# An attention, feed-forward and mixture-of-experts block: the first batch's tokens are chosen inside the tile loop, and four experts run batch by batch on raw fp32 weights

## The chip, the cores and the metric

One core of a Trainium2 chip. The time is that of one execution on the device, in microseconds. The engines: PE (TensorE, matmul), DVE (VectorE), ACT (ScalarE), POOL (GpSimd) and SP (SyncE, which here only issues DMAs). Each engine takes its instructions in the order of the program and waits at semaphores for the others.

## The reference

Two batches of 2048 rows of 512 values (x) pass four residual blocks; each begins with a layer norm.

```python
x = x + xattn0(layernorm(x), ctx, ctx, mask, ...)   # q, k, v and scores with relu, no softmax
x = x + ffn0(layernorm(x), weight, bias)            # input and weight rounded to blocks of fp6
x = x + xattn1(layernorm(x), ctx, W, b)             # a matmul and a mean of ctx
x = x + moe(layernorm(x), Wg, bg, w1, ..., b3)

# moe, for each of 16 experts e and each batch b
probs = softmax(x @ Wg + bg, axis=-2)               # over the 2048 rows
vals, idx = top_k(probs.T, 128)                     # 128 rows for each expert
h = relu(tok @ w1[e] + b1[e]); h = relu(h @ w2[e] + b2[e]); h = h @ w3[e] + b3[e]
outputs[b, idx] += h * vals                         # tok = x[b, idx]
```

Each expert takes the 128 rows of each batch that it rates highest. An expert's top rows aren't known before the last of the batch's 2048 rows has its logits.

## The kernel before

Rows are worked on in N = 32 tiles of 128; tiles 0 to 15 are the first batch. A loop over k = 0 to 35 is software-pipelined, written once for each engine: iteration k quantises tile k (`quantise`), adds the feed-forward result of tile k-1, mixes tile k-2 (`mix` on PE), and ends tile k-3 (`second_residual` on DVE). Ahead run the q projection (`q_chunk`), `scores` for groups of four tiles, and `attend(k+1)` with `first_residual(k+1)`. Each residual is followed by its statistics (bn_stats and bn_aggr on DVE, or sums on ACT), from which POOL makes a reciprocal root (`rstd_of`). DVE also takes the low part of each value that goes through PE in three passes: a value is split in a high and a low part (fp32r), and a product is high x high, high x low and low x high (`three_passes`, L250). `xdT_l` is that low part for the quantised tile, and the feed-forward matmuls `ffn(k)` wait for it. Some choices of order depend on k: from tile 24 on `attend(k+1)` stands ahead of the transposes `t2(k)` (`ahead`), and at k = 27 behind the mix (`mix_first`).

Each group of four tiles writes its logits into `seg`: a row for each batch, expert and quarter of 512 rows, 128 rows in all; the first batch's are rows 0 to 63 and complete in iteration 19. The normed rows go to the tensor xn4 in DRAM, the sums of the first three blocks to out.

Behind the loop each engine waits for all of this (`phase1_over`). Then DVE chooses: 16 rounds of max, max_index and match_replace give the 128 largest of each row of 512; the four quarters are brought into one row by a DMA (`cand`) and merged by a bitonic network (L1486 to L1513). PE turns ids and values (L789, L791), and POOL gathers the tokens by indirect DMA (L1714). The expert stage takes expert by expert, both batches together, 256 tokens: `hidden(e, 0)`, the transposes of the next expert's tokens, `outputs(e-1)`, `hidden(e, 1)`. Weights, 1 MB for a layer, come by DMA into `w_raw`, ACT and DVE split them into `w_h` and `w_l`. The results are added to out by an indirect DMA on POOL (L1725). `keep_warm` are matmuls whose result nobody reads.

## Time and profile before

| | |
|---|---|
| median of 3 runs | 786.26 us (785.6 to 787.0) |
| profiled execution | 786.69 us |
| its span, first to last instruction | 784.9 us |
| PE busy | 698.9 us (89%) |
| DVE busy | 554.4 us (71%) |
| ACT busy | 446.6 us (57%) |
| POOL busy | 436.5 us (56%) |
| mean granted clock of PE | 0.954 |
| moved by DMA | 103.04 MB, mean 131 GB/s |

The span is what the trace covers; the execution's own time is 1.8 us longer. The granted clock is a share of 2.4 GHz and has two levels, 1.00 and 0.50. Busy shares are means over stages that are quite different, so the sections below go by stage.

### The profile page before, as it was taken

Reading aid. Unit: us, or ns where it says so; the run is one execution under the profiler, and the core shown is the slowest. Engines: PE = TensorE matmul, PEld = TensorE weight load, DVE = VectorE, ACT = ScalarE, POOL = GpSimd, SP = SyncE. Lnnn points to the kernel's source line nnn. Section 1 sums busy time; section 2 is a strip of 40 time slices with the busy share of each in tenths; the row PEclk is TensorE's granted clock in tenths of the full one; section 3 lists DMA queues with packets and bytes.
Section 4 is the critical chain, followed back from the end, with each engine's and each line's share of the span. In section 5 each row is a group of like instructions: output and inputs, shape, how many; then the busy total and the mean of one; then the engine's idle time right before and its main releaser. Section 6 shows DMA issues by size and latency. Waiting matters only on the chain.

```text
span 784.9 us, 12400 instructions
## 1 busy us (share of the span) xinstructions
PE 698.9 (89%) x4357; PEld 617.7 (79%) x4357; DVE 554.4 (71%) x918; ACT 446.6 (57%) x750; POOL 436.5 (56%) x596
## 2 busy tenths in 40 slices
PE   6999999999999999999883007999999999999993
PEld 5766888888888888888772006999999999999993
DVE  5787588788787978777775984576666767677741
ACT  5754677777777676545352203656566666665640
POOL 2635788888888888877672603044444333334321
PEclk9999999999999999999897557999999999999998
DMA  8600122222212221111114144278888878777742
GB/s 306 236 28 14 42 95 67 83 68 83 81 56 96 68 87 52 65 45 56 41 70 158 71 167 126 91 225 242 240 247 235 236 239 238 234 226 220 216 66 35
DMA packets 54093, 103.04 MB, mean 131 GB/s; under 512 B 5392, under 2 KB 6672, under 8 KB 54032
## 3 DMA queue, kind: packets, MB, share of 16 engines
q1 hardware_dynamic: 46864, 85.47, 33.3%
q0 software_dynamic: 7168, 16.78, 9.6%
q8 instruction: 35, 0.57, 0.3%
q14 instruction: 26, 0.21, 0.1%
HBM read 76.68 MB, written 25.17 MB: 130 GB/s over the span
## 4 chain that ended last, share of the span: by engine, by line
PE 54%; DVE 13%; ACT 11%; issue 9%; POOL 9%; DMA 2%; POOLq 0%; SPq 0%; ACTq 0%; DVEq 0%
PE bank L250 31%; PE banks L250 12%; PE bank L257 4%; ACT xn L927 3%; POOL rstd_all L1603 3%; DVE bn L1155 2%; DVE x L1316 2%; PE banks L571 2%; PE banks L577 1%; DVE pack L1432 1%; DVE left L1439 1%; ACT qT_h L960 1%; DVE pos L1434 1%; POOL x L1690 1%; POOL xd L1682 1%
## 5 line engine op out<-in xcount | busy, mean ns | idle before, releaser
L1725 POOL DMA_INDIRECT out<-y,ids x32 | 76.2, 2380 | 173.6 <-DVE y L1552 169.0
L1167 DVE TENSOR_TENSOR w_l<-w_raw,w_h 128x2048 fp32r<-128x2048 f32 x45 | 103.0, 2290 | 31.2 <-ACT w_h L871 30.0
L1118 ACT ACTIVATE h<-bank,b 128x512 f32<-128x512 f32 x64 | 44.0, 687 | 107.5 <-PE bank L250 107.5
L871 ACT ACTIVATE w_h<-w_raw 128x2048 fp32r<-128x2048 f32 x48 | 90.6, 1924 | 5.3 <-DMA w_raw<-w 5.3
L1167 DVE TENSOR_TENSOR hT_l<-h,hT_h 128x512 fp32r<-128x512 f32 x64 | 44.2, 691 | 66.9 <-ACT hT_h L1124 66.9
L250 PE MATMUL bank<-hT_h,w_l 128*128 128x256 f32 x256 | 72.4, 283 | 0.0
L250 PE MATMUL bank<-hT_h,w_h 128*128 128x256 f32 x256 | 72.4, 283 | 0.0
L250 PE MATMUL bank<-tokT_h,w_h 128*128 128x256 f32 x256 | 72.4, 283 | 0.0
L250 PE MATMUL bank<-tokT_l,w_h 128*128 128x256 f32 x256 | 72.4, 283 | 0.0
L250 PE MATMUL bank<-hT_l,w_h 128*128 128x256 f32 x256 | 72.4, 283 | 0.0
L250 PE MATMUL bank<-tokT_h,w_l 128*128 128x256 f32 x256 | 72.4, 283 | 0.0
L1155 DVE BATCH_NORM_STATS2 bn<-x 128x6 f32<-128x512 f32 x79 | 54.6, 691 | 7.5 <-DMA x<-x 5.2
L1714 POOL DMA_INDIRECT tok<-xn,ids x32 | 31.9, 998 | 47.6 <-DVE ids L1522 29.4
L250 PE MATMUL bank<-wf_h,xdT_h 128*128 128x512 f32 x128 | 53.0, 414 | 0.8 <-DVE xdT_l L1167 0.8
L250 PE MATMUL banks<-w_h,hT_h 128*128 128x512 f32 x128 | 51.2, 400 | 0.0
L250 PE MATMUL bank<-wf_h,xdT_l 128*128 128x512 f32 x128 | 50.3, 393 | 0.0
L250 PE MATMUL bank<-wf_l,xdT_h 128*128 128x512 f32 x128 | 50.0, 391 | 0.0
L250 PE MATMUL banks<-w_h,hT_l 128*128 128x512 f32 x128 | 49.9, 390 | 0.0
L250 PE MATMUL banks<-w_l,hT_h 128*128 128x512 f32 x128 | 49.8, 389 | 0.0
L250 PEld LDWEIGHTS bank<-hT_l,w_h 128*128 128x128 f32 x256 | 49.1, 192 | 0.6
L250 PEld LDWEIGHTS bank<-hT_h,w_h 128*128 128x128 f32 x256 | 49.1, 192 | 0.6
L250 PEld LDWEIGHTS bank<-tokT_h,w_h 128*128 128x128 f32 x256 | 49.1, 192 | 0.2 <-issue 0.2
(249 smaller groups left out, 2233.1 us busy)
## 6 DMA issues: line engine op xcount, KB each, us to landing
w_raw<-w SPq DMA_DIRECT2D x48, 1024.0 KB, 6.9
x<-x SPq DMA_DIRECT2D x32, 256.0 KB, 2.8
out<-x SPq DMA_DIRECT2D x32, 256.0 KB, 2.0
xn<-xn SPq DMA_DIRECT2D x32, 256.0 KB, 2.0
mask<-mask_t SPq DMA_DIRECT2D x8, 256.0 KB, 3.1
stage<-wk SPq DMA_DIRECT2D x1, 1024.0 KB, 7.9
stage<-wq SPq DMA_DIRECT2D x2, 512.0 KB, 7.9
stage<-wf SPq DMA_DIRECT2D x1, 1024.0 KB, 10.9
```

The costliest lines, as they stand in the source:

```text
L250: last = pe.matmul(out, a, b, start=(n == 0), stop=(n == 3 * len(pairs) - 1))
L257: last = pe.transpose(bank[:, c * P:(c + 1) * P], src[:, c * P:(c + 1) * P], ident[:, :])
L571: last = pe.matmul(both_halves[:, a, 0:WIDE], xh[:, d, :], wc_h[:, d, a, :], start=(d == 0), stop=(d == C - 1))
L871: act.activation(dst, src, ACT.Copy).then_inc(sem, 1)
L927: act.activation(spare[:, :], src[:, :], ACT.Copy, scale=-1.0 / D, accum_out=m[:, 0:1]).then_inc(sm.a_sum, 1)
L1118: act.activation(h32[n % 2][:, :], ps_hid[n % 4][:, :], ACT.Relu, bias=bias)
L1155: dve.bn_stats(bn6[which][:, j % 2, :], src[:, :]).then_inc(sem_bn[which], 1)
L1167: dve.tensor_tensor(dst, src, hi_part, ALU.subtract).then_inc(sem, 1)
L1316: dve.scalar_tensor_tensor(x1[j % 2][:, :], ps_av[:, :], 0.0, x_in[j % XR][:, :], ALU.max, ALU.add)\
L1603: pool.tensor_tensor(inverse, r[:, 0:1], eps_exp[:, :], ALU.pow).then_inc(sem, 1)
L1714: pool.indirect_dma_start(out=tok[e % 2][:, b, :], out_offset=None, in_=io.xn4, in_offset=bass.IndirectOffsetOnAxis(ap=ids[:, r:r + 1], ax ...
L1725: pool.indirect_dma_start(out=out_rows, out_offset=bass.IndirectOffsetOnAxis(ap=ids[:, r:r + 1], axis=0), in_=y[e % 2][b][:, :], in_offset ...
```

## The change

The first batch's choice moves into the loop. `top_step(0, n)`, n = 0 to 47, are the 48 instructions of the 16 rounds on rows 0 to 63: five in each of the iterations 20 to 27, then 3, 3 and 2. `load_cand(0)` brings the lists together, and the merge's ten steps stand in iterations 31 (three), 32 (three) and 33 (four). The ids are turned in iterations 34 and 35, and the first four tokens' gathers are issued before `phase1_over` is passed or right behind it. The statistics of the third residual of tiles 19 to 30 (`THIRD`) are made on ACT (`sums3`) instead of on DVE. `mix_first` goes: attend(28) and first_residual(28) stand where they do in the other iterations, and quantise(28) comes first in its iteration on DVE.

The second batch's choice stays behind the loop, on rows 64 to 127 alone.

Experts 0 to 3 no longer go through three passes. They run batch by batch in 24 units (2 batches, 4 experts, 3 layers; `gap_of`), two experts alternating. A unit is four transposes, a copy to SBUF on ACT (`gap_in`), four fp32 matmuls of 128x512 with the weights as they come from DRAM (`gap_layer`), and an eviction on ACT (`gap_out`). The first 12 units belong to the first batch. Each unit loads its weights anew, so 24 loads where the four experts had 12; four are issued in iterations 28 to 31. Experts 4 to 15 run as before (ES = 12). keep_warm of the expert stage goes, and the last outputs begin with the first two of four chunks while the others are still made (`last_outputs`).

```diff
+    THIRD = range(19, 31)
+    STEPS = 3 * TOP // 8
+    def steps_of(k):
+        if 20 <= k < 28:
+            return range(5 * (k - 20), 5 * (k - 19))
+        return {28: range(40, 43), 29: range(43, 46), 30: range(46, STEPS)}.get(k, [])
+    def gap_of(n):
+        return n // 12, 2 * (n // 6 % 2) + n % 2, n // 2 % 3, n % 2
...
+        def load_gap(n):
+            b, e, layer, s = gap_of(n)
+            if n >= 4:
+                sp.wait_ge(sm.p_gl, n - 3)
+            else:
+                sp.wait_ge(sm.p_q, N)
+            sp.dma_start(gw[n % 4][:, :, :], chunked(io.w[layer][e])).then_inc(sem_gw[n % 4], 16)
...
         for i in range(RAW):
             load_raw(i)
-        sp.wait_ge(sm.k_top, 1)
-        sp.wait_ge(sm.a_soft, 1)
-        sp.dma_start(cand[:, :, :], pack[:, :]).then_inc(sm.k_cand, 16)
-        for i in range(RAW, len(order)):
+        for n in range(4, 10):
+            load_gap(n)
+        load_cand(1)
+        for n in range(10, 14):
+            load_gap(n)
+        for i in range(RAW, 2 * RAW):
+            load_raw(i)
+        for n in range(14, GAP):
+            load_gap(n)
+        for i in range(2 * RAW, len(order)):
             load_raw(i)
...
+        gap_turn(0)
+        for n in range(GAP):
+            gap_layer(n, 0)
+            if n + 1 not in (12, GAP):
+                gap_turn(n + 1)
+            gap_layer(n, 1)
+            if n + 1 == 12:
+                ids_turned(1, ps[1])
+                vals_turned(1, ps[0])
+                gap_turn(12)
+            if n == GAP - 2:
+                tokens(0)
+        for e in range(ES):
             hidden(e, 0)
-            if e == 0:
-                keep_warm(8, wh, ps_y[0])
...
             if parts_of(k) is not None:
                 logit_parts(parts_of(k))
+            for n in steps_of(k):
+                top_step(0, n)
+            if k == 30:
+                top_closed(0)
             if valid(k):
                 dve.wait_ge(sm.a_hi2, k + 1)
                 lo(sm.d_lo2, xd_l[:, :, :], in4(ps_tb), xd_h[:, :, :])
...
-            if not ahead(k) and valid(k + 1) and not mix_first(k):
+            if k == N - 1:
+                merge_open(0)
+                for i in range(3):
+                    merge_step(0, i)
+            if not ahead(k) and valid(k + 1):
                 first_residual(k + 1)
```

The order on DVE in iteration 20, from the add of tile 19's feed-forward result to the statistics of tile 21's first residual. Before:

```order
L1391 TENSOR_TENSOR x_1_125<-bank,x_1_134 128x512
L1155 BN_STATS bn_71<-x_1_125 128x6
L1160 BN_AGGR mean_var_67<-bn_71 128x2
L1167 TENSOR_TENSOR xdT_l<-bank,xdT_h 128x512
L1316 SCALAR_TENSOR_TENSOR x_1_134<-bank,x_98 128x512
L1155 BN_STATS bn_70<-x_1_134 128x6
L1160 BN_AGGR mean_var_66<-bn_70 128x2
L1330 SCALAR_TENSOR_TENSOR x_0_140<-banks,rstd_all_54,x_0_124 128x512
```

Now (the numbers in names differ from program to program):

```order
L1750 TENSOR_TENSOR x_1_133<-bank,x_1_142 128x512
L1611 MAX pack<-seg_logits 64x8
L1619 TENSOR_SCALAR negm<-pack 64x1
L1621 MATCH_REPLACE left_153<-pack,seg_logits 64x512
L1611 MAX pack<-left_153 64x8
L1615 MAX_INDEX pos<-pack,seg_logits 64x8
L1407 TENSOR_TENSOR xdT_l<-bank,xdT_h 128x512
L1558 SCALAR_TENSOR_TENSOR x_1_142<-bank,x_106 128x512
L1395 BN_STATS bn_70<-x_1_142 128x6
L1400 BN_AGGR mean_var_66<-bn_70 128x2
```

The statistics behind the add are gone, and five steps of the choice (the small negm belongs to the third) stand between the add and xdT_l.

The order on DVE in iteration 24, where `attend` and the first residual stand ahead. Before:

```order
L1316 SCALAR_TENSOR_TENSOR x_1_134<-bank,x_102 128x512
L1155 BN_STATS bn_70<-x_1_134 128x6
L1160 BN_AGGR mean_var_66<-bn_70 128x2
L1167 TENSOR_TENSOR xdT_l<-bank,xdT_h 128x512
L1339 TENSOR_REDUCE amax<-xc 128x16
```

Now:

```order
L1558 SCALAR_TENSOR_TENSOR x_1_142<-bank,x_110 128x512
L1395 BN_STATS bn_70<-x_1_142 128x6
L1400 BN_AGGR mean_var_66<-bn_70 128x2
L1621 MATCH_REPLACE left_153<-pack,left_152 64x512
L1611 MAX pack<-left_153 64x8
L1615 MAX_INDEX pos<-pack,left_152 64x8
L1621 MATCH_REPLACE left_154<-pack,left_153 64x512
L1611 MAX pack<-left_154 64x8
L1407 TENSOR_TENSOR xdT_l<-bank,xdT_h 128x512
L1585 TENSOR_REDUCE amax<-xc 128x16
```

The five steps stand between the new statistics and xdT_l, for which PE's next ffn waits.

The order on PE where the loop ends: lg_t are the last logits, top_i and top_v ids and values, tok the tokens. Before:

```order
L789 MATMUL bank<-ident,top_i 128x32
L791 MATMUL bank<-ident,top_v 128x32
L470 MATMUL banks<-w_h_186 128x512 x7
L257 MATMUL bank<-ident,tok_196 128x128 x8
L470 MATMUL banks<-w_h_186 128x512 x8
```

Now, from the values of the first batch on:

```order
L833 MATMUL banks<-ident,top_v_194 128x16
L289 MATMUL bank<-ident,gap_tok_176 128x128 x4
L932 MATMUL bank<-gap_w_202,gap_xT_178 128x512 x2
L289 MATMUL bank<-ident,gap_tok_177 128x128 x4
L932 MATMUL bank<-gap_w_202,gap_xT_178 128x512 x2
L932 MATMUL bank<-gap_w_203,gap_xT_179 128x512 x2
L289 MATMUL bank<-ident,gap_h_180 128x128 x4
L932 MATMUL bank<-gap_w_203,gap_xT_179 128x512 x2
```

And at the border of the two batches:

```order
L932 MATMUL bank<-gap_w_205,gap_xT_179 128x512 x4
L828 MATMUL bank<-ident,top_i_197 128x16
L833 MATMUL bank<-ident,top_v_195 128x16
L289 MATMUL bank<-ident,gap_tok_176 128x128 x4
L932 MATMUL bank<-gap_w_202,gap_xT_178 128x512 x2
```

Units follow each other on PE, the transposes of the next in the middle of each; the ids of the second batch are turned behind the twelfth unit, and its first tokens behind them.

## Rows read from the trace of the kernel before

**Rows 1.** Stages: start:end, us, busy us of PE, PEld, DVE, ACT, POOL, clock, DMA, GB/s.

```profile
281.94:327.07 45.13, 45.02 (x263) 39.04 (x262) 36.14 (x66) 28.30 (x60) 37.45 (x61) 1.00 0.21 70
327.07:367.72 40.65, 40.07 (x235) 35.14 (x234) 30.29 (x60) 20.62 (x44) 32.66 (x52) 1.00 0.15 56
367.72:425.57 57.85, 44.51 (x262) 38.93 (x260) 38.65 (x79) 22.54 (x50) 33.70 (x61) 0.92 0.18 65
425.57:479.96 54.39, 3.92 (x9) 2.50 (x9) 46.22 (x148) 7.24 (x7) 16.87 (x7) 0.50 0.36 127
479.96:772.87 292.91, 292.87 (x2076) 275.71 (x2076) 186.67 (x172) 176.36 (x205) 103.13 (x60) 1.00 0.72 205
```

**Rows 2.** The chain that ended last, expert stage: start us, us, what.

```profile
483.50 5.75 PE bank L250 x48
...
491.96 11.52 PE bank L250 x96
503.48 0.87 PE bank L257 x8
504.35 5.47 PE banks L250 x24
...
764.64 2.75 PE bank L470 x12
```

**Rows 3.** Timeline of the hole: start us, us, engine, instruction, [idle before].

```profile
425.57 0.69 DVE L1432 MAX8 pack<-seg_logits 128x8 f32<-128x512 f32 x1 [3.31 <-DMA seg_logits<-lrow]
...
457.79 0.29 DVE L1444 TENSOR_SCALAR pack<-pos,segbase 128x128 f32<-128x128 uint32 x1
460.96 0.15 DVE L1449 TENSOR_REDUCE gmax<-cand 32x1 f32<-32x4 f32 x1 [2.89 <-DMA cand<-pack]
...
474.76 0.28 PE L789 MATMUL bank<-ident,top_i 32*128 32x32 f32 x1 [52.15 <-DVE es L1516]
...
479.96 1.38 PE L257 MATMUL bank<-ident,tok 128*128 128x128 f32 x5 [0.38 <-DMA tok<-xn,ids]
```

**Rows 4.** Source line 619: duration ns, first and last start us, forms.

```profile
L619 PE MATMUL banks<-stage,ctx_raw x8: 592/592/595, 33.7 to 36.7; 128*128 128x512 f32 x8
```

**Rows 5.** Three short stretches, columns as in rows 1.

```profile
372.30:375.40 3.10, 0.00 (x0) 0.00 (x0) 2.96 (x7) 1.24 (x3) 2.47 (x6) 1.00 0.01 3
375.40:382.20 6.80, 6.09 (x27) 6.09 (x28) 4.80 (x11) 1.35 (x3) 4.99 (x9) 0.50 0.11 41
...
476.30:481.20 4.90, 4.53 (x13) 3.10 (x14) 0.00 (x0) 0.08 (x1) 3.46 (x4) 0.50 0.54 144
```

**Rows 6.** Timeline of DVE in iteration 20 of the tile loop.

```profile
286.81 0.68 DVE L1391 TENSOR_TENSOR x<-bank,x 128x512 f32<-128x512 f32 x1
...
288.26 0.18 DVE L1160 BATCH_NORM_AGGREGATE mean_var<-bn 128x2 f32<-128x6 f32 x1
290.26 0.69 DVE L1167 TENSOR_TENSOR xdT_l<-bank,xdT_h 128x512 fp32r<-128x512 f32 x1 [1.81 <-ACT xdT_h L871]
...
292.53 0.75 DVE L1330 SCALAR_TENSOR_TENSOR x<-banks,rstd_all,x 128x512 f32<-128x512 f32 x1
```

**Rows 7.** Timeline of DVE and PE in iterations 24 and 25.

```profile
333.67 0.69 DVE L1316 SCALAR_TENSOR_TENSOR x<-bank,x 128x512 f32<-128x512 f32 x1 [1.22 <-PE bank L250]
...
343.70 0.69 DVE L1316 SCALAR_TENSOR_TENSOR x<-bank,x 128x512 f32<-128x512 f32 x1 [1.77 <-PE bank L250]
...
337.26 0.48 PE L250 MATMUL bank<-wf_h,xdT_h 128*128 128x512 f32 x1
```

**Rows 8.** DMA issues (KB, us to landing), and a stretch with three loads.

```profile
w_raw<-w SPq DMA_DIRECT2D x48, 1024.0 KB, 6.9
...
430.50:433.70 3.20, 0.00 (x0) 0.00 (x0) 3.13 (x9) 1.91 (x1) 0.97 (x1) 0.50 1.04 391
```

**Rows 9.** Timeline of DVE: the same instruction in two iterations.

```profile
355.30 1.08 DVE L1297 TENSOR_TENSOR lg_sum<-lt 128x128 f32<-128x128 f32 x1
...
420.86 0.27 DVE L1297 TENSOR_TENSOR lg_sum<-lt 128x128 f32<-128x128 f32 x1
```

More of the change, by code:

```diff
@@ L58, in build @@
     SEG = G * E
-    ROWS = B * E
+    NG = 4
+    ES = E - NG
     CB = B * KEYS
@@ L124, in build @@
     wgf = place("wg_pair", [P, C, 2 * E])
-    ids = place("ids", [P, ROWS], U32)
-    vals = place("vals", [P, ROWS])
+    ids = place("ids", [P, B * E], U32)
+    vals = place("vals", [P, B * E])
+    b3v = place("b3_vals", [P, B * E])
+    negm = place("negm", [P, 1])
+    gmax = [place(f"gmax{b}", [E, 4]) for b in range(B)]
+    eg = [place(f"eg{b}", [E, GB]) for b in range(B)]
+    es = [place(f"es{b}", [E, GB]) for b in range(B)]
     phase_base = top[0]
@@ L166, in build @@
     xn4 = [place(f"xn4_{i}", [P, D]) for i in range(2)]
+    left = [place(f"left{i}", [P, GT]) for i in range(3)]
+    pos = place("pos", [P, TOP], U32)
+    pack = place("pack", [P, 2 * TOP + 1])
+    assert top[0] <= at_cd + 16 * 1024
     top[0] = at_cd + 16 * 1024
@@ new lines, in build @@
+    exps = place("exps", [P, GT], at=at_xn1)
+    spot = [at_q32]
+    top_v = [more(f"top_v{b}", [E, TOP]) for b in range(B)]
+    top_i = [more(f"top_i{b}", [E, TOP]) for b in range(B)]
+    y = [[more(f"y{i}{b}", [P, D]) for b in range(B)] for i in range(2)]
+    assert spot[0] <= at_xt1
+    gw = [place(f"gap_w{i}", [P, C, D], at=at_xt1 + 8 * KB * i) for i in range(4)]
+    w_h += [place(f"w_h{3 + i}", [P, C, D], F32R, at=at_xt1 + 8 * KB * i) for i in range(2)]
+    w_l += [place(f"w_l{3 + i}", [P, C, D], F32R, at=at_xt1 + 8 * KB * (2 + i)) for i in range(2)]
@@ L217, in banks @@
+    h32 = [more(f"h32_{i}", [P, 2 * B * P]) for i in range(2)]
+    h_h = [more(f"hT_h{i}", [P, C, B * P], F32R) for i in range(2)]
+    h_l = [more(f"hT_l{i}", [P, C, B * P], F32R) for i in range(2)]
+    assert spot[0] <= at_cd + 8 * KB, (spot[0], at_cd + 8 * KB)
     def banks(*names):
@@ L765, in _ @@
                 t2(k)
-            if valid(k + 1) and not ahead(k) and not mix_first(k):
+            if valid(k + 1) and not ahead(k):
                 attend(k + 1)
@@ L1352, in quantise, with top_step @@
                 .then_inc(sm.d_q8, 1)
+        def top_step(b, n):
+            rows = rows_of(b)
+            r = n // 3
+            now = (seg if r == 0 else left[r % 3])[rows, :]
+            eight = pack[rows, 8 * r:8 * r + 8]
+            if n == 0 and b == 0:
+                for i in range(2):
+                    dve.wait_ge(sem_seg[i], 16 * (G // 4))
+            if n % 3 == 0:
+                chain[0] += 1
+                dve.max(eight, now).then_inc(sm.d_chain, 1)
+                max_at[0] = chain[0]
+            if n % 3 == 1 and r >= 1:
+                last = (seg if r == 1 else left[(r - 1) % 3])[rows, :]
+                dve.max_index(pos[rows, 8 * r - 8:8 * r], pack[rows, 8 * r - 8:8 * r], last)
+            if n % 3 == 2:
+                dve.wait_ge(sm.d_chain, max_at[0])
+                if r == 0:
+                    dve.tensor_scalar(negm[rows, :], pack[rows, 0:1], -1.0, None, ALU.mult).then_inc(sm.k_exp, 1)
+                if r + 1 < TOP // 8:
+                    then(dve.match_replace(left[(r + 1) % 3][rows, :], eight, now, LOWEST))
+                else:
+                    then(dve.max_index(pos[rows, 8 * r:8 * r + 8], eight, now))
@@ L1556, in _ @@
         nxt = AHEAD
-        for e in range(E):
+        for e in range(ES):
             if nxt < len(order):
```

548 lines of the change are left out of this document (373 added, 175 removed).

## The prediction

> **What bounds the kernel now.** I read the busy time by stage first, then the chain that ended last, then the rows of single stages.
>
> [Rows 1] give three kernels in one. In the tile loop PE is busy 45.02 of 45.13 us over four tiles, so PE sets the pace; DVE is busy 36.14 of them. Between 425.57 and 479.96 PE works 3.92 us of 54.39: everything waits for the choice of the tokens, on DVE. From 479.96 PE is busy 292.87 of 292.91 us, the DMA engines 0.72. The reader should see that PE has one hole, and that DVE, whose work the hole waits for, still has some room in the loop.
>
> In the expert stage the chain is PE alone, 11.52 + 0.87 + 5.47 = 17.86 us an expert [rows 2]; warm-up matmuls stand in front of the last outputs (2.75 us).
>
> In the hole [rows 3]: 48 steps of eight, from 425.57 to 457.79, 0.671 us each; lists in another layout by DMA at 460.96; after the merge PE turns the ids at 474.76; the gathered tokens are on PE at 479.96. That is 54.39 us for both batches together. Each instruction is charged by elements in a row, not by rows, so I take one batch alone (64 rows for 128, 16 lists for 32) at the same time. That is a choice; no row shows an instruction on fewer partitions against the same one on more.
>
> **The change part by part, against the profiled span of 784.9 us** (786.69 us as a run, 0.4 over the median).
>
> *Fewer three-pass experts.* Four of sixteen go: 4 x 17.86 = **-71.4**. The warm-up matmuls go too: before the last outputs 2.75, behind the first hidden layer eight more (about 1.8, by the same 0.23 us each). Splitting the last outputs by halves lets their first half, 2.7 us, hide the ReLU and the low part of the second: **-4.6**, and +0.3 because both batches' results now end closer together.
>
> *Raw fp32 layers.* A layer is four transposes and four 128x512 fp32 matmuls. Eight hardware passes for four such matmuls start from 33.7 to 36.7 [rows 4], 0.43 apart, so 3.43 us; eight transposes take 0.87 [rows 2], so four 0.43. A unit is 3.86 us on PE; four experts, two batches, three layers make 24 units, 92.6 us, more than the 71.4 they replace. The gain is only in where they lie. ACT's copies fit: the turn of the next unit stands in the middle of a layer, 1.7 us away from either end, and two evictions take about 0.7 each.
>
> *First batch: hidden.* Its 12 units run while DVE chooses for the second. They end at 0.8 + 12 x 3.43 + 11 x 0.43 + the cold clock. The granted clock was 0.50 after the loop and came back 4.9 us after PE resumed [rows 5]; I charge 2.5 us. With about 1 us of start that is 50.1 us after the loop. The second batch's ids come at 0.9 (DVE now first waits for PE's turn of the first values) + 49.2 [rows 3]. So it is a tie: nothing is exposed, nor is there any cover left. From here each us that the first 12 units lose is an us of the total. I add **+1.2** for the 0.9 and the tie.
>
> *Second batch: exposed.* Its ids are as late as before, then 12 units run where before the experts began. Before, 3.5 us lay from the first transposes to the first hidden layer at 483.50 [rows 2]. Now 0.4 + 0.8 + 12 x 3.43 + 11 x 0.43 = 47.1, + 0.9 for the tokens of the first normal expert. PE also idles 4.8 us for the gather. An idle of 3.84 us in the loop brought the clock to 0.50 for 6.8 us [rows 5], so I charge 2.5 again: 50.5 - 3.5 = **+47.0**.
>
> *The tile loop.* DVE gets 48 steps and the first merge; twelve bn_stats/bn_aggr pairs move to ACT, which has 17 us free over four tiles. Iteration 20: the pair ended at 288.44, then DVE waited 1.81 for ACT before xdT_l, and x of the next tile began at 292.53 [rows 6]. Now five steps (3.36) begin at 287.5 where the pair stood: -0.95 + 3.36 - 1.81 = +0.6. Over iterations 20 to 23 DVE needs 36.14 + 20 x 0.67 - 4 x 0.95 = 45.8 of 45.13 us, plus waits that steps can't fill. Walked row by row I get **+1.9**.
>
> From iteration 24 attend(k+1) stands ahead, and the steps lie between the new first residual and xdT_l, on which PE's next ffn waits. The old period is 343.70 - 333.67 = 10.03 [rows 7]. The new circle is: ffn start to first residual 343.70 - 337.26 = 6.44, the residual and its statistics 1.65, steps 3.36, xdT_l 0.7: 12.2. Three such iterations, **+6.6**. DVE's idle of 10.4 us in that stage [rows 1] doesn't help, since it waits for PE's attend ahead of the steps.
>
> Iterations 27 and 28: PE had idled 3.84 us and then ran 6.8 us at half clock [rows 5], because first_residual(28) stood behind the mix. Now it stands right behind xdT_l, but eight more steps do too: walked from xdT_l of tile 26, the transposes of tile 28 start as late as before (18.3 us on), the idle time in smaller parts. What goes is the half clock, 2.5 us over the mix; 1.0 is lost again where ffn(28) waits for xdT_l: **-1.5**. In iterations 29 and 30 the circle of [rows 7] still holds, with five steps and the close of the lists in it, 3.36 + 0.29, less 0.2: **+3.4**. Iterations 31 to 34 take the merge, 13.5 of the 13.8 us from 460.96 to 474.76 [rows 3]. DVE waits in them mostly for the last mixes (idle 19.2 of 57.85 us in this stage, [rows 1]). By my walk some 10 us of the merge fill such waits; its last four steps end 1.9 us behind the last mix, and 1.3 is lost before: **+3.2**. The merge can also be held by POOL. lg_sum took 1.08 us in one place and 0.27 in another [rows 9]; at the first a POOL tensor instruction ran beside it. In iterations 31 to 33 POOL has five long ones (three biases, xd, one x1), so 5 x 0.8 = 4 us at most, and I take **+1.0**.
>
> The Trainium skill (GPSIMD Engine Reference, section Key points) says that GpSimd shares its SBUF interfaces with VectorE, with contention for instructions that have two SBUF inputs. By it all of the merge's some 60 two-input instructions in the loop are exposed, and the search instructions, with one tensor input, are not; the trace agrees for lg_sum. If each of them met a POOL instruction the loop would grow by 60 x 0.8, some 48 us, and the kernel would be slower, 820.
>
> The loop in sum: 1.9 + 6.6 - 1.5 + 3.4 + 3.2 + 1.0 = **+14.6**. Bounds: all steps into idle time and only what exceeds it paid, some +4; and every step and merge paid in full, 48 x 0.67 + 13.5 - 12 x 0.95 = +34. I take the walk, as each of its terms names the instruction that waits.
>
> *Transfers.* 24 loads of 1 MB for four experts, since each batch loads them anew. Three loads ran at 391 GB/s (2.7 us each), landing 6.9 us after issue in the median [rows 8]. A unit needs 1.05 MB and a sixth of a megabyte of gathers and adds, 3.2 to 3.5 us of engines in 3.86. Four loads start in the loop, the others when a buffer is free, three units ahead (11.6 us for a landing of 6.9). I cost them at nothing; the cover is that 0.4 us a unit.
>
> **Sum:** 784.9 - 71.4 - 4.6 + 0.3 + 1.2 + 47.0 + 14.6 = 772.0; a run 1.8 more, against a median 0.4 lower: **773.4 us**.
>
> **The rivals.**
>
> *A. The loop absorbs the choice.* For it: DVE's idle, 9.0 and 10.4 us, covers the 9.6 net of four tiles, and iteration 28's stall returns 6 us. Against it: the wait for attend lies ahead of the steps. Loop +0 to +8, central 4: 763.
>
> *B. Slower: the weights feed doesn't keep up.* Between units a load must arrive every 3.86 us, 1.22 MB with its share of gathers and adds. The expert stage moved 205 GB/s at 0.72 [rows 1]. If something near 235 GB/s were the ceiling for this mix a unit would be 5.2 us, and as the tie leaves no cover all 24 pay: + 1.35 x 24 = 32, so 806. It decides from 0.54 us a unit, a unit of 4.4. Against it: 391 GB/s at the loads [rows 8].
>
> *C. The loop pays in full.* Every step lands on the path, +34, and idle PE brings the clock down again: 793. It decides from a stretch of 27. For it: DVE reaches 100% of the loop's pace; against: [rows 6] shows waits that steps fill.
>
> *D. The clock stays at 1.2 GHz in the fp32 units.* A unit would be 7.7 us, some +85. The fp32 rows ran at full pace [rows 4]. Nearly excluded.
>
> *E. Held by POOL.* Each instruction of the merge in the loop is held 0.8 us: 820, as five POOL instructions can't do; 0.01.
>
> *F. The clock never falls between the batches,* or the tie is won: 2 to 3 us less, within the range.
>
> By the Trainium skill (TensorE: Matmul & The Clock Gate, section HAM oscillation) gaps of idle throttle the engine again. By that rule the 4.8 us before the second batch costs what [rows 5] shows, and the sum already holds it; were PE's small waits in iterations 24 to 30 (0.7 to 2.5 us) enough, each would cost some 3 us more.
>
> **How the numbers follow.** My forecast, loop +8 to +21: 0.62. A 0.18. C, loop over +21: 0.08, a third of it still slightly faster or level. B and other stalls of the units: 0.10, a part of it (below 0.5 us a unit) still faster. D and E 0.02. A measurement of this kernel tells about 0.2% (1.6 us) from no change. Faster: 0.62 + 0.18 + 0.03 + 0.04 = 0.87; same 0.03; slower 0.10. The range takes in A's centre and the lower part of B and C: 761 to 785.
>
> **What the new profile would show.** PE busy in units of 3.9 us for some 50 us after the loop, a hole of 5 us, 47 us of units, then twelve periods of 17.86. The last logits landing near 440 instead of 425.57. In iterations 24 to 26 PE waiting about 2 us each for xdT_l. Wrong would be: transposes or fp32 matmuls waiting on gap_w (B), the loop ending before 433 (A) or after 447 (C), a search instruction that gets dearer or cheaper on 64 partitions.

## The result: slower by 1%, where 1.6% faster was forecast

Median 794.14 us (793.88 to 794.93, 4 runs) against 786.16 (785.6 to 787.0, 4 runs): ratio 1.0102, 95% interval 1.0085 to 1.0120. The profiled execution has a span of 791.8 us, where my sum gave 772.0. The page of the changed kernel:

```profile
span 791.8 us, 12063 instructions
...
PE 724.0 (91%) x4100; PEld 596.2 (75%) x4100; DVE 544.7 (69%) x1000; ACT 451.7 (57%) x807; POOL 429.4 (54%) x596
...
PEclk9999999999999999999989799789999999999997
```

I read the windows by stage next, against [rows 1]; columns as there.

```profile
292.52:332.22 39.70, 36.91 (x205) 31.58 (x204) 37.10 (x71) 25.13 (x57) 27.32 (x45) 0.96 0.14 48
332.22:370.82 38.60, 32.09 (x176) 27.35 (x174) 30.33 (x66) 21.44 (x47) 26.58 (x43) 0.96 0.13 48
370.82:387.01 16.19, 14.09 (x69) 12.25 (x70) 12.61 (x29) 6.67 (x15) 7.39 (x14) 0.89 0.29 100
387.01:420.35 33.34, 26.89 (x146) 23.31 (x144) 24.88 (x57) 16.54 (x39) 19.90 (x36) 0.90 0.43 142
420.35:451.64 31.29, 15.81 (x103) 13.65 (x104) 25.03 (x90) 11.11 (x27) 15.04 (x23) 0.89 0.25 87
451.83:512.56 60.73, 50.16 (x147) 24.55 (x147) 50.53 (x151) 23.41 (x40) 23.95 (x11) 0.89 0.95 318
512.56:563.65 51.09, 50.40 (x153) 25.23 (x153) 1.29 (x2) 15.98 (x25) 10.48 (x9) 0.93 0.76 242
```

The first five are the tile loop from iteration 21 on, then the first batch's units, then the second's. The reader should see two things. In the loop DVE is nearly full at first (37.10 of 39.70) and PE no longer is. And the last logits land at 451.64 instead of 425.57 [rows 3]; the second batch's tokens are on PE at 512.56:

```profile
451.64 0.25 PE L833 MATMUL banks<-ident,top_v 16*128 16x16 f32 x1 [4.60 <-DMA seg_logits<-lrow]
...
512.56 1.11 PE L289 MATMUL bank<-ident,gap_tok 128*128 128x128 f32 x4 [6.45 <-DMA gap_tok<-xn,ids]
```

Four stages against the forecast:

| stage | forecast | measured | miss |
|---|---|---|---|
| last logits landed | 440.2 | 451.64 | +11.5 |
| from there to the second batch's tokens on PE | 55.6 | 60.9 | +5.3 |
| from there to the first three-pass matmul | 50.5 | 51.1 | +0.6 |
| from there to the end | 225.7 | 228.1 | +2.4 |

### The profile page after: what moved, and what is told of

The parts are those of the page before. It is cut to its first block, busy times and chain, and to the rows that moved or that the text cites. A ratio compares the mean times of both kernels' runs of the same rounds, so it can differ in the third digit from the quotient of the medians.

```text
span 791.8 us, 12063 instructions
## 1 busy us (share of the span) xinstructions
PE 724.0 (91%) x4100; PEld 596.2 (75%) x4100; DVE 544.7 (69%) x1000; ACT 451.7 (57%) x807; POOL 429.4 (54%) x596
## 4 chain that ended last, share of the span: by engine, by line
issue 23%; PE 21%; DVE 18%; DMA 15%; POOL 11%; ACT 10%; POOLq 0%; DVEq 0%; ACTq 0%; SPq 0%
DMA out<-y,ids 13%; PE bank L282 7%; PE bank L932 5%; POOL rstd_all L1893 3%; PE bank L289 2%; ACT xn L1094 2%; DVE bn L1395 2%; DVE left L1621 2%; DVE pos L1615 2%; DVE pack L1611 2%; DVE x L1558 1%; PE banks L282 1%; POOL x L1980 1%; POOL xd L1972 1%; ACT qT_h L1153 1%
## 5 line engine op out<-in xcount | busy, mean ns | idle before, releaser
L2015 POOL DMA_INDIRECT out<-y,ids x24 | 56.2, 2341 | 131.4 <-DVE y L1837 127.7
L1407 DVE TENSOR_TENSOR w_l<-w_raw,w_h 128x2048 fp32r<-128x2048 f32 x33 | 75.6, 2290 | 26.5 <-ACT w_h L1038 26.5
L932 PE MATMUL bank<-gap_w,gap_xT 128*128 128x512 f32 x192 | 91.0, 617 | 1.5 <-ACT gap_xT L1308 1.5
L1407 DVE TENSOR_TENSOR hT_l<-h,hT_h 128x512 fp32r<-128x512 f32 x48 | 33.2, 691 | 50.9 <-ACT hT_h L1346 49.4
L932 PEld LDWEIGHTS bank<-gap_w,gap_xT 128*128 128x128 f32 x192 | 36.1, 199 | 37.6 <-issue 35.1
L1038 ACT ACTIVATE w_h<-w_raw 128x2048 fp32r<-128x2048 f32 x33 | 62.2, 1926 | 0.0
L282 PE MATMUL bank<-hT_h,w_h 128*128 128x256 f32 x192 | 54.3, 283 | 1.4 <-DVE hT_l L1407 1.4
L282 PE MATMUL bank<-wf_l,xdT_h 128*128 128x512 f32 x128 | 51.1, 399 | 0.0
L1034 ACT ACTIVATE xn<-x,rstd,rstd_all 128x512 f32<-128x512 f32 x32 | 26.2, 818 | 31.0 <-POOL rstd L1895 30.7
L1034 ACT ACTIVATE xn<-x,rstd 128x512 f32<-128x512 f32 x32 | 26.1, 816 | 30.9 <-POOL rstd L1901 24.8
L1904 POOL TENSOR_TENSOR qT_l<-q,qT_h 128x512 fp32r<-128x512 f32 x32 | 41.5, 1299 | 3.5 <-ACT qT_h L1153 3.5
L1407 DVE TENSOR_TENSOR xdT_l<-bank,xdT_h 128x512 fp32r<-128x512 f32 x32 | 21.9, 685 | 30.2 <-ACT xdT_h L1038 30.0
```

Source lines behind the costliest of these rows:

```text
L282: last = pe.matmul(out, a, b, start=(n == 0), stop=(n == 3 * len(pairs) - 1))
L932: last = pe.matmul(ps[4 + s][:, :], gx[s][:, d * P:(d + 1) * P], gw[n % 4][:, d, :], start=(d == 0), stop=(d == C - 1))
L1034: act.activation(dst[:, :], src[:, :], ACT.Identity, bias=r[:, n, 2:3], scale=scale)\
L1038: act.activation(dst, src, ACT.Copy).then_inc(sem, 1)
L1407: dve.tensor_tensor(dst, src, hi_part, ALU.subtract).then_inc(sem, 1)
L1904: pool.tensor_tensor(dst, src, hi_part, ALU.subtract).then_inc(sem, 1)
```

## The experiments

**Theories.** Mine after reading the trace, in two places. In the loop, the steps ahead of `xdT_l` keep PE's feed-forward waiting (9.7 us on the page where it was 0.8), and from iteration 28 the moved statistics stand in a circle through ACT and POOL. In the hole, one comparison of the second batch's merge took 4.19 us beside a split on POOL. Rivals: the changed order of PE and DVE did it; or DVE is simply full, so that no order helps; or the comparison was slow of itself.

All in all fourteen kernels. Each was timed beside the kernel before, whose median was 786.1 to 786.5 us every time, so their medians can be compared. late_choice and stats_back have one execution each. The yardstick in the loop is the start of `second_residual`, the add that ends tile k-3, one per iteration; the table gives the time between two of them, from the profiled execution of each kernel:

| | 21 to 24 | 24 to 27 | 27 to 28 | 28 to 31 | 31 to 34 | sum |
|---|---|---|---|---|---|---|
| before | 34.5 | 30.7 | 9.9 | 32.9 | 18.6 | 126.7 |
| after | 39.7 | 38.6 | 16.2 | 33.3 | 23.2 | 151.1 |
| late_choice | 33.9 | 31.1 | 15.8 | 33.3 | 20.1 | 134.1 |
| order_back | 39.7 | 38.6 | 14.5 | 37.0 | 23.2 | 153.0 |
| stats_back | 39.7 | 38.2 | 19.1 | 28.1 | 23.7 | 148.8 |
| stats_short | 39.4 | 38.7 | 19.1 | 28.1 | 23.7 | 148.9 |
| steps_behind | 39.7 | 33.3 | 15.8 | 33.3 | 23.4 | 145.4 |
| split_early | 39.6 | 40.2 | 19.0 | 33.3 | 25.3 | 157.5 |
| combined | 39.4 | 33.3 | 15.8 | 28.1 | 24.6 | 141.2 |
| combined_all | 41.5 | 32.7 | 16.0 | 28.1 | 23.8 | 142.0 |
| fewer_steps22 | 37.3 | 34.9 | 15.8 | 29.9 | 23.7 | 141.6 |

Split_early alters nothing in the loop, so its row against that of the changed kernel (after) tells how far two executions of one loop lie apart: 1.6 us in iterations 24 to 26, 2.9 in 27, 2.1 in 31 to 33, and next to nothing in 21 to 23 and 28 to 30. Smaller differences in those columns say nothing.

### late_choice: the choice taken out of the loop

```diff
-            for n in steps_of(k):
-                top_step(0, n)
...
         phase1_over(dve)
+        for n in range(STEPS):
+            top_step(0, n)
...
```

> The first batch's 48 steps, its merge and its turned ids and values stand behind the tile loop, ahead of the second batch's; everything else as in the changed kernel, the moved statistics and the altered order included. It is no candidate: it prices what the choice itself costs inside the loop. My theory: of the loop's +25.9 us, some 18 to 22 are the steps and the merge, and 4 to 8 are the moved statistics (the circle of iterations 28 to 31); so the loop ends 4 to 8 us behind the kernel before, at 429 to 434, and the profiled span is 791.8 - 25.9 + 6 + 55 (the first choice, exposed) = about 827. Rival: the moved statistics and the order cost most of it: the loop ends at 440 or later, and the span is 836 or more.

Span 826.3 us, as expected. DVE's first step starts right behind the last logits:

```profile
433.24 0.69 DVE L1603 MAX8 pack<-seg_logits 64x8 f32<-64x512 f32 x1 [3.51 <-DMA seg_logits<-lrow]
```

That is 7.7 us behind the kernel before. It is the price of what the change leaves in the loop without the choice: the moved statistics, the altered order and the four early loads; no run takes these apart. Its PE waits 0.7 us in all for `xdT_l`, like before. Against it the changed kernel is 18.4 us later (451.64), and that is the choice in the loop. Of the 17.0 us between the two rows of the table 13.3 lie in iterations 21 to 26, 3.1 in 31 to 33, and only 0.5 in 27 to 30, where the circle leaves DVE time anyway.

### steps_behind: the steps of iterations 24 on behind xdT_l

```diff
-            for n in steps_of(k):
+            for n in steps_of(k) if k < 24 else []:
                 top_step(0, n)
             if valid(k):
                 dve.wait_ge(sm.a_hi2, k + 1)
                 lo(sm.d_lo2, xd_l[:, :, :], in4(ps_tb), xd_h[:, :, :])
+            for n in steps_of(k) if k >= 24 else []:
+                top_step(0, n)
             if k == 30:
                 top_closed(0)
-            if valid(k):
-                dve.wait_ge(sm.a_hi2, k + 1)
-                lo(sm.d_lo2, xd_l[:, :, :], in4(ps_tb), xd_h[:, :, :])
```

> From iteration 24 the five steps stand behind VectorE's low part of the turned tile (xdT_l), on which TensorE's next feed-forward waits, instead of ahead of it. My theory: the steps then fill VectorE's wait for ScalarE's centred tile and TensorE's waits for xdT_l go, about 1 to 1.5 us in each of iterations 24 to 30: the loop ends 5 to 10 us earlier and the median is about 787. Rival: VectorE is simply full in iterations 22 to 27 and what it does not do here it does there: the loop ends within 2 us of the changed kernel's 451.6 and the median stays at 793 to 795.

788.5 us (787.53 to 789.82, 9 runs), 5.6 less than the changed kernel; ratio to the kernel before 1.0026 (1.0016 to 1.0037). Iterations 24 to 26 take 33.3 instead of 38.6 us, and PE's waits for `xdT_l` shrink. The rows of the two pages, after and steps_behind:

```profile
L282 PE MATMUL bank<-wf_h,xdT_h 128*128 128x512 f32 x128 | 54.4, 425 | 9.7 <-DVE xdT_l L1407 9.6
```

```profile
L282 PE MATMUL bank<-wf_h,xdT_h 128*128 128x512 f32 x128 | 53.1, 415 | 2.3 <-DVE xdT_l L1407 2.3
```

So place, not load, made 5.3 us of it: the same 15 steps cost 7.5 us ahead of `xdT_l` (38.6 against late_choice's 31.1) and 2.2 behind it. In iterations 28 to 30 nothing changed, so there the steps aren't what binds.

### stats_short and stats_back: the moved statistics

```diff
-    THIRD = range(19, 31)
+    THIRD = range(19, 27)
```

(stats_back leaves THIRD empty.)

> The third statistics of tiles 27 to 30 go back from ScalarE to VectorE; those of tiles 19 to 26 stay moved. My theory: in iterations 28 to 31 of the changed kernel the pace (11.1 us) is set by a circle through ScalarE's two sums and GpSimd's reciprocal root behind them, not by VectorE's load: the period of iterations 28 to 30 falls to 9.5 to 10.3 although VectorE has 0.95 us more in each, and the median falls by 2 to 5, to about 790. Rival: VectorE's load sets the pace there too, then each of the four iterations gets 0.9 us longer and the median is about 797.

> All twelve third statistics are back on VectorE; the steps and everything else as in the changed kernel. My theory: VectorE is full in iterations 20 to 27, so each of these grows by 0.7 to 0.95 us, some 6 in all, while iterations 28 to 31 lose the circle and get 3 to 5 shorter: 793 to 798 in total. Rival: VectorE was not what bound iterations 20 to 27, the moved sums on ScalarE and the reciprocal root at the end of GpSimd's turn were: then the loop ends 5 us or more earlier and the time is below 790.

792.07 (791.72 to 792.86) and 791.97 (one run). Both take 28.1 us for iterations 28 to 30 instead of 33.3, although DVE has more to do. So the moved statistics held these iterations, not DVE's load. The way that they do it I read from the rows of the changed kernel, around iteration 28:

```profile
391.83 0.27 POOL L1895 TENSOR_SCALAR rstd<-mean_var,rstd_all 128x1 f32<-128x1 f32 x1
392.13 0.81 ACT L1034 ACTIVATE xn<-x,rstd,rstd_all 128x512 f32<-128x512 f32 x1 [2.17 <-POOL rstd L1895]
392.85 0.61 ACT L1094 ACTIVATE v_bias<-x 128x512 f32<-128x512 f32 x1
393.59 0.73 ACT L1096 ACTIVATE v_bias<-x,mean_var 128x512 f32<-128x512 f32 x1
394.31 0.71 ACT L1207 ACTIVATE xc<-x,mean_var 128x512 f32<-128x512 f32 x1
394.49 0.19 POOL L1880 TENSOR_SCALAR rstd<-mean_var 128x1 f32<-128x1 f32 x1 [2.39 <-ACT v_bias L1096]
395.05 0.69 DVE L1585 TENSOR_REDUCE amax<-xc 128x16 f32<-128x512 f32 x1 [1.73 <-ACT xc L1207]
396.39 0.23 POOL L1899 TENSOR_SCALAR rstd<-rstd 128x1 f32<-128x1 f32 x1
```

POOL's root lets ACT norm; ACT's two sums (1.46 us) stand ahead of `xc`, for which DVE waits 1.73; POOL does the third root (from 394.49) ahead of the one that the quantising needs (396.39). Then DVE quantises, POOL makes xd and adds two biases, and the next root comes 11.1 us later. TensorE's clock, a rival for these 5.2 us, is not the cause: in the changed kernel iteration 28 took 11.14 us at a granted 1.00 and 29 took 11.11 at 0.85.

For iterations 20 to 26 my theory fell: stats_back puts 0.95 us per tile back on DVE there, and iterations 21 to 26 take no longer (39.7 and 38.2 against 39.7 and 38.6). Iteration 20 took 11.5 us instead of 10.5, but it took 11.2 in stats_short, which alters nothing there. By this one execution these statistics had been moved for nothing. In both kernels iteration 27 took 19.1 us against the changed kernel's 16.2; split_early, with the changed kernel's loop unaltered, shows 19.0 too, so that need not be the edit (see the last section).

### order_back: the order of iteration 27

```diff
-        return ahead(k) and k > N - 8
+        return ahead(k) and ahead(k - 1)
+    def mix_first(k):
+        return scores_of(k) is not None and not q_units(k)
...
```

> The two rules of order that the change altered are put back as they were: the attention of tile 28 behind the mix of iteration 27 on TensorE, its first residual at the start of the next iteration on VectorE, and the statistics of the last normalisation behind the quantising only where the tile before is ahead too. The steps and the moved statistics stay. My theory: order is not what cost the time; the half clock behind the long wait at iteration 27 comes back and the median is 794 to 797. Rival: the altered order is what stretches iterations 27 to 30, and the median falls by 4 to 8, to about 788.

795.76 us (793.31 to 797.75), 1.6 more, with overlapping ranges; iterations 27 to 30 take 51.5 us instead of 49.5, and 52.4 in split_early with the changed kernel's own order. The rival wanted 4 to 8 us less, so the order is not the cause; whether the new one is any better isn't shown.

### split_early: POOL's split ahead of the merge

```diff
         gap_add(0, 0)
+        split_lo(2)
         gap_add(0, 1)
-        split_lo(2)
```

> One line moved: GpSimd's low part of the third weight matrix stands ahead of the first batch's second scatter-add instead of behind it. My theory: in the changed kernel that split (486.86 to 491.93) held VectorE's first merge comparison of the second batch, 4.19 us instead of about 0.5 (488.02 to 492.21). Now the split should run from about 481.4 to 486.4, beside search instructions that read one tensor, and end ahead of the merge. The comparison takes about 0.5 us, the second batch's first unit starts at about 508.5 instead of 512.56, and the median falls by 4, from 794.1 to about 790. Rival: the comparison was slow because its lists had just landed by DMA, or because 16 partitions with strides are slow: it still takes 4 us and the time stays at 794.

The changed kernel, DVE and POOL:

```profile
488.02 4.19 DVE L1657 TENSOR_TENSOR ge<-cand 16x256 f32<-16x256 f32 x1
492.14 0.41 DVE L1663 TENSOR_TENSOR list_v<-cand 16x256 f32<-16x256 f32 x1
...
486.86 5.07 POOL L1904 TENSOR_TENSOR w_l<-w_raw,w_h 128x2048 fp32r<-128x2048 f32 x1
```

and split_early:

```profile
495.45 0.40 DVE L1657 TENSOR_TENSOR ge<-cand 16x256 f32<-16x256 f32 x1
...
488.13 4.51 POOL L1904 TENSOR_TENSOR w_l<-w_raw,w_h 128x2048 fp32r<-128x2048 f32 x1 [1.51 <-ACT w_h L1298]
```

4.19 against 0.40 us for the same instruction, the lists just landed in both: POOL's instruction held it until its own end at 491.93. In steps_behind and stats_short, where the split stands as in the changed kernel, it took 4.12 and 3.59. The first batch's units to the second batch's tokens take 57.15 instead of 60.73 us. The Trainium skill (SBUF — State Buffer, section SBUF: two separate sides) calls this an exclusive lock for the whole instruction and not a shared bandwidth; the trace agrees. The search steps ran on beside POOL's splits, 0.69 us as elsewhere. The median did not move (794.09, 792.62 to 797.13). In the profiled execution, the slowest of the four, iterations 21 to 33 took 6.4 us longer than in the changed kernel with the same loop, so a gain of 3.6 was not to be told in four runs. It stands by its rows, and by combined's, where the stretch from the last logits to these tokens is 57.1 us instead of 60.9.

### combined, combined_all, fewer_steps22

Combined is steps_behind, stats_short and split_early. Combined_all puts every step behind the first residual at the iteration's end; fewer_steps22 deals the steps out as `{20: 5, 21: 5, 22: 2, 23: 5, 24: 6, 25: 6, 26: 6, 27: 4, 28: 3, 29: 3, 30: 3}`.

> Three of the edits together: the steps of iterations 24 on behind xdT_l, the third statistics of tiles 27 to 30 back on VectorE, and GpSimd's third split ahead of the second scatter-add. If the causes are separate they add up: the loop ends at 451.6 - 4.1 - 3.5 = 444, the first unit of the second batch comes 57 us after the first of the first, and the median is 794.1 - 5.6 - 2.0 - 3.6 = 783, under the kernel before (786.3). Rival: the first two are one gain seen twice, as what iteration 26 gives back is lost in iterations 27 and 28: 786 to 788.

> As combined, but every step, those of iterations 20 to 23 too, stands behind xdT_l and behind the next tile's first residual and its statistics, at the end of VectorE's iteration. My theory: in iteration 22 TensorE waits 2.29 us for xdT_l behind three steps and then runs 4.29 us for 3.0 at half clock; these go, 3 to 5 us over iterations 20 to 23, and the median is 778 to 781. Rival: VectorE is full there in any case (11 us busy of 11.3) and the delay only moves on to the next tile's third residual: within 1.5 us of combined.

> Combined, with the 48 steps dealt out anew over iterations 20 to 30: 5, 5, 2, 5, 6, 6, 6, 4, 3, 3, 3 instead of 5 in each of the first eight and 3, 3, 2. Iteration 22 also has the three sums for the logits on VectorE; there the kernel without any step in the loop had a period of 10.5 us and combined one of 14.4. My theory: the steps ahead of xdT_l make TensorE wait and fall to half clock, so iteration 22 gets back 2 to 3.5 us; one step more in each of iterations 24 to 26 costs at most 0.7 us each, since they lie behind xdT_l: the loop ends 1.5 to 3 us earlier and the median is 777 to 778.5 against 779.9. Rival: VectorE is full from 20 to 27 whatever the order, and the three steps come back in full, so the time is the same within 1.

Combined: 779.92 us (779.13 to 781.39), ratio 0.9920 (0.9907 to 0.9934). The causes add up, and the kernel is faster than before. It gains 14.2 us on the changed kernel where the three by themselves make 11.2; in combined iteration 27 took 15.8 us, as in steps_behind, where the two others had 19.0 and 19.1. Combined_all: 783.11 (782.89 to 784.71), 3.2 worse: iteration 20 grows from 10.5 to 13.3 us and 21 to 23 from 39.4 to 41.5. Fewer_steps22: 781.0 (780.3 to 782.39). It wins 2.0 us where the steps left and loses 3.4 where they went. Its loop ends with combined's (the third residual of iteration 34 begins at 433.99 in both). So in iterations 20 to 23 DVE is full, another order doesn't help, and what leaves there is paid elsewhere: there the rival was right. Combined_all has no wait of PE for `xdT_l` there and is slower even so. 5.5 us of the choice stay (39.4 against late_choice's 33.9).

### warm_gap, raw_later: clock and transfers behind the hole

First warm_gap's edit to combined, then raw_later's:

```diff
                 vals_turned(1, ps[0])
+                pe.wait_ge(sm.a_w, 3)
+                keep_warm(22, w_h[2], ps[6])
                 gap_turn(12)
```

```diff
-        for n in range(10, 14):
+        for n in range(10, 18):
             load_gap(n)
         for i in range(RAW, 2 * RAW):
             load_raw(i)
-        for n in range(14, GAP):
+        for n in range(18, GAP):
             load_gap(n)
```

> Combined, with 22 matmuls of 512 columns that compute nothing needed, on TensorE between the turn of the second batch's values and its first tokens (some 4.8 us of the 6.5 us in which it is idle). It prices the term of 2.5 us for the clock behind that hole. My theory: the second batch's units run at full clock from the first on, the 51.8 us from the first transposes on become 49 to 49.5, and the median falls by 2 to 2.5, to 777.5. Rival: the idle time is not what lowers the clock (the fp32 units themselves are), or the added work reaches beyond the tokens' landing: then no gain.

> Combined, with the loads of the fourth to sixth three-pass weight matrices (3 MB) behind the second batch's first units' loads in SyncE's queue instead of ahead of them, issued at about 511 instead of 485.5. Combined's gather of the second batch's first tokens took 6.2 us from the copy of the ids to the transposes, with the DMA engines busy all the time. Theory: these 3 MB in flight delay the gather, so it takes 4.5 us, the second batch starts 1.5 to 2 us earlier and the median is about 778. Rival: the loads for the next units fill the DMA engines just as well: no change, or a unit of the second batch waits for its weights.

Both against combined. Warm_gap: 780.06 (779.36 to 781.03), no gain. The clock did stay at full; combined, then warm_gap:

```profile
499.20:504.00 4.80, 4.11 (x8) 2.12 (x9) 0.00 (x0) 0.60 (x1) 2.25 (x2) 0.50 1.05 387
```

```profile
500.50:505.00 4.50, 3.81 (x16) 2.07 (x16) 0.00 (x0) 1.19 (x2) 2.74 (x3) 1.00 1.04 387
...
510.65 1.96 PE L932 MATMUL bank<-gap_w,gap_xT 128*128 128x512 f32 x4 [0.77 <-issue]
515.85 0.67 PE L932 MATMUL bank<-gap_w,gap_xT 128*128 128x512 f32 x1 [1.08 <-issue]
```

The last two rows are waits inside units 14 and 15; combined has none there. They gave 1.85 us of it back, and the second batch's stretch, from its first transposes to the first three-pass matmul, took 50.3 us instead of 50.9. Raw_later: 787.17 (784.77 to 788.61), 7.3 worse. The gather was no faster (6.5 us from the copy of the ids to the transposes, combined 6.6), and a unit waited where the loads had moved to:

```profile
531.37 2.05 PE L932 MATMUL bank<-gap_w,gap_xT 128*128 128x512 f32 x2 [4.24 <-issue]
```

Behind that wait PE ran at a granted 0.58 for 6.7 us. My theory fell in this form: these three loads are not what holds the gather. The DMA share stayed at 1.05 during it (492.90 to 499.40), and loads put off from there are missed later.

### raw_early, raw_early_warm, one_early_warm

Raw_early issues the three loads ahead of those for units 8 and 10 and behind the lists; raw_early_warm adds 18 warm-up matmuls; one_early_warm has those and only the first of the loads early. Its edit of the loads:

```diff
         for n in range(4, 10):
+            if n == 8:
+                load_raw(RAW)
             load_gap(n)
...
-        for i in range(RAW, 2 * RAW):
+        for i in range(RAW + 1, 2 * RAW):
             load_raw(i)
```

> Combined, with the loads of the fourth to sixth three-pass weight matrices issued earlier: ahead of the loads for units 8 and 10 and right behind the lists, instead of one after the other at 485.5. In combined the DMA engines are busy 0.74 to 0.80 of the time from 462 to 482 and 1.04 to 1.07 from 482 to 522, across the gather of the second batch's tokens. My theory: transfers are a cost around that gather; with 3 MB moved into the quieter stretch the gather takes about 5 us instead of 6.1 and the median is 1 to 2 us under combined's 779.9. Rival: the loads only trade places, the stretch of 482 to 522 stays full, and the time is the same within 0.7.

> Raw_early and 18 matmuls that compute nothing needed in the wait for the second batch's tokens. With 22 of them and the old order of loads the clock stayed at full, but TensorE then waited 0.77 and 1.08 us inside units 14 and 15, and the second batch's stretch went only from 50.9 to 50.3. My theory: those waits were for weights behind a full set of DMA engines; with the earlier loads they go, the stretch is 48.5 to 49, and the median is 776 to 778. Rival: the waits were TensorE's own (the turn of the hidden rows behind ScalarE), they stay, and the time is that of raw_early.

> Combined, with 18 warm-up matmuls in the wait for the second batch's tokens and only one of the three weight loads earlier (ahead of unit 8's, at about 463); none is added between 466 and the lists' transfer at 476. In raw_early the lists' transfer took 10.4 us instead of 2.4, with some 6 MB issued in the 15 us ahead of it, while the gather fell from 6.1 to about 4 us. My theory: what is in flight at the moment a small transfer is issued sets how long it takes; here the lists take under 4 us and the gather 5 to 6, so the median is 778 to 780. Rival: any load moved into the first batch's units holds the lists, and the median is above 782.

Raw_early: 787.34 (785.43 to 789.58), 7.4 worse than combined. The second batch's lists, 64 KB, issued at 478.40, were there only at 488.77:

```profile
488.77 0.15 DVE L1647 TENSOR_REDUCE gmax<-cand 16x1 f32<-16x4 f32 x1 [12.07 <-DMA cand<-pack]
...
478.40 0.71 SPq L525 DMA_DIRECT2D cand<-pack  x1
```

In combined they took 2.4:

```profile
478.54 0.15 DVE L1646 TENSOR_REDUCE gmax<-cand 16x1 f32<-16x4 f32 x1 [2.47 <-DMA cand<-pack]
...
476.10 0.59 SPq L525 DMA_DIRECT2D cand<-pack  x1
```

The gather did fall, to 4.0 us from the copy of the ids. But it came so much later that most loads were through: the DMA share during it was 0.37, where it was 1.06 in combined. So this gain goes with the delay, and one load moved early alone (one_early_warm) didn't bring it.

Raw_early_warm: 786.27 (784.9 to 788.15). PE had idled 8.27 us just before the ids were turned; the warm-ups behind that ran at half clock for the most part (granted 0.50 until 506), 6.75 us for 18. The tokens' transposes began at 508.98, 7.2 us behind the copy of the ids instead of 4.0. One_early_warm: 777.79 us (776.98 to 778.15), ratio 0.9892 (0.9875 to 0.9908), the fastest kernel here:

```profile
500.00:547.90 47.90, 47.20 (x151) 23.70 (x152) 1.29 (x2) 15.97 (x25) 11.73 (x10) 1.00 0.84 271
...
494.78 4.39 PE L580 MATMUL banks<-w_h 128*128 128x512 f32 x18
500.01 0.66 PE L289 MATMUL bank<-ident,gap_tok 128*128 128x128 f32 x4 [0.84 <-DMA gap_tok<-xn,ids]
```

From the tokens to the first three-pass matmul 48.0 us, against combined's 50.9: the warm clock is worth 2.9 when the weights are there, as combined has no wait for weights in this stretch either. Its tokens came 0.8 us later, which leaves the 2.1 of the median. The lists took 2.4 us again, as I expected, but the gather 6.6 as in combined, not 5 to 6: the whole gain is the clock's. Why such warm-ups (22 of them) gave next to nothing in warm_gap I read as the one load that is now earlier, since the two waits in units are gone; it wasn't tried by itself. That loads issued shortly ahead of the lists hold them is shown for the orders tried, not where the bound lies. The Trainium skill (DMA: Bandwidth & Descriptors, section Queues, rings and completion order) has a transfer's completion land on each DMA engine only behind that engine's earlier writes. The 10.4 us agree with it, and would as well if the lists' own data had waited behind the loads; no run tells the two apart.

## Why the prediction was wrong

It failed in the step "The loop in sum: +14.6". The loop got 26.1 us longer, which is rival C's case by its size (over +21), to which I gave 0.08. It is not C's mechanism: C lets every step be paid, and late_choice shows 0.1 us for those of iterations 28 to 30. That C's 793 is so near the measured 794 is luck; it has +34 for the loop, and nothing for the hole. Where I wrote "by my walk" the prediction doesn't show the walk, so that for +1.9, -1.5 and +3.2 only the result of the step can be named. By the terms (starts of `second_residual` against before):

- **Iterations 20 to 23, +1.9: measured +5.2.** I let DVE be full (45.8 of 45.13 us) and still paid only 1.9, as if the steps could fill all but that little of its waits. The steps stand ahead of `xdT_l`. In iteration 22 the logit sums come ahead of them as well. DVE's and PE's rows and a window of PE's next matmuls there:

```profile
310.01 1.20 DVE L1538 TENSOR_TENSOR lg<-lg_sum,rstd_all 128x64 f32<-128x64 f32 x1
311.24 1.22 DVE L1540 TENSOR_TENSOR lg<-lg,lg_sum 128x64 f32<-128x64 f32 x1
...
316.98 0.50 PE L282 MATMUL bank<-wf_h,xdT_h 128*128 128x512 f32 x1 [2.29 <-DVE xdT_l L1407]
...
317.00:321.30 4.30, 4.30 (x13) 3.43 (x14) 4.13 (x8) 2.75 (x7) 2.28 (x4) 0.67 0.16 61
```

  Two sums took 1.2 us each where they take 0.23 elsewhere, PE waited 2.29 us, and its granted clock then was 0.67 on the mean of 4.3 us. late_choice, without steps, waits 0.7 us in all. Yet none of these three by itself makes the +5.2: in stats_back both sums take 0.23 us and the clock stays at 1.00, combined_all has no such wait, and iterations 21 to 23 take 39.7 and 41.5 us all the same. What these runs have in common is the steps on a nearly full DVE (busy 37.10 of 39.70 us here, 38.3 of 39.6 in stats_back); fewer_steps22, with three steps less in iteration 22, gets back 2.0 us, their own length.
- **Iterations 24 to 26, +6.6: measured +7.9.** Mechanism right, size nearly: PE waited 1.37, 1.91 and 3.12 us for `xdT_l`, where I had said about 2 each. steps_behind shows the place and takes 5.3 of it back.
- **Iterations 27 and 28, -1.5: measured +2.6.** Wrong in sign. I had credited 2.5 us for a half clock that goes. It didn't: the granted clock was 0.89 in iteration 27 and 0.90 in 28 to 30. late_choice has +2.1 there without a step, and split_early, with the same loop, 2.9 more for iteration 27. How the rest divides between the order and the moved statistics was not tried.
- **Iterations 29 and 30, +3.4: measured +4.1, by another cause.** I charged the steps. They cost nothing (late_choice has the same period of 11.1 us); the moved statistics, which I had taken as cost-free on ACT's 17 us of idle time, hold these iterations (stats_short takes 5.2 us less for 28 to 30). Idle time of an engine says nothing on whether it is idle at that place of the circle.
- **Iterations 31 to the end, +3.2 and +1.0: measured +6.3.** By late_choice 1.6 of it is not the merge. How the rest divides was not tried.

**The hole, "So it is a tie" and the 5.2 of the gather: +5.3.** The units themselves were right: 3.87 us each against 3.86. I looked for POOL's hold on the merge in the loop (E, +1.0) and not in the hole, where one split holds one instruction: +3.6 by split_early. The gather took 7.5 us from the turned ids instead of 5.2, beside DMA engines that are full (share 1.06; before, 0.38): +2.3. Together that is 5.9 for a miss of 5.3. That full DMA engines make the gather longer rests on these rows and on raw_early's 4.0 us at 0.37; no run changed that alone. "I cost them at nothing", said of the transfers, was right for the units of the changed kernel, which waited for no weights, and wrong for small transfers beside them.

**The second batch, +47.0: right** (51.1 against 50.5), the 2.5 us for the clock included: 2.9 by one_early_warm. Three-pass experts, -71.4 and -4.6: the last stage is 2.4 us longer than summed. The step that failed is the 1.8 credited for the eight warm-up matmuls behind the first hidden layer. They had stood in a wait that stays:

```profile
572.24 0.36 PE L282 MATMUL bank<-hT_h,w_h 128*128 128x256 f32 x1 [1.41 <-DVE hT_l L1407]
```

From the first three-pass matmul to the transposes of the third expert's tokens the changed kernel takes 20.17 us (563.65 to 583.82) and the kernel before, warm-ups included, 19.81 (483.50 to 503.31): +0.4 where the sum has -1.8.

Rival A (+0 to +8) is excluded: in combined, with the steps placed better, the loop still ends 16.5 us later than before, at 442.06. B did not occur, but raw_later (4.24 us in one unit) shows how near it lies. D and E did not occur; F only where warm-ups were added.

## What to carry to other kernels

Before work is put into a filled loop, ask not whether the engine has room but what waits behind the place: the same 15 steps cost 7.5 us ahead of the operand that TensorE waits for and 2.2 us behind it. Price each helping edit alone too: what the change left in the loop without the choice, statistics on another engine, a new order and early loads, cost 7.7 us and was credited with a gain. Warm-up matmuls that stand in a wait cost nothing, so taking the eight out gained nothing. Where a hole is filled with work that loads megabytes and splits weights, look at the small transfers and the two-input vector instructions on the path next to it: moving a few lines and adding 18 warm-up matmuls took this kernel from 794.1 to 777.8.

## What the runs showed of the hardware

- Search instructions on 64 partitions cost what they do on 128: 0.67 to 0.69 us for a row of 512 (MAX8, FIND_INDEX8, MATCH_REPLACE8), in split_early beside a 4.5 us split on POOL too. A comparison of two SBUF tensors took 4.19 instead of 0.40 us beside such a split.
- Where the clock falls differs between executions of the same loop. The same stretch of iteration 27 in the changed kernel and in split_early, whose loop is the same:

```profile
370.82:379.00 8.18, 6.19 (x28) 4.93 (x28) 5.67 (x14) 4.70 (x11) 4.28 (x7) 1.00 0.17 64
```

```profile
373.01:381.00 7.99, 7.86 (x22) 6.28 (x23) 4.17 (x10) 2.46 (x6) 3.87 (x6) 0.61 0.17 66
```

  The iteration took 16.2 us in the one and 19.0 in the other; with the steps behind `xdT_l` it was 15.8 to 16.0 in every profile.
- A 64 KB transfer took 2.4 us with three or four loads of 1 MB issued in the 15 us ahead of it, the last 5.8 us before or more (after, combined, one_early_warm); 5.5 with four, the last 2.1 us before (late_choice); and 10.4 with five in the 15 us ahead and two more in the us before those, the last 0.5 us before it (raw_early). How much is the number of loads and how much the distance of the last one no run tells.
- A gather's first tokens came 4.0 us behind the copy of the ids at a DMA share of 0.37, and 6.5 to 7.1 us at 1.05 to 1.06.
